# Row statistics in two GpSimd instructions an iteration, and six tiles of rows normalised on ScalarE

## What is computed

```python
x = x + xattn(layernorm(x), ctx)          # 16 heads, 8-bit q, k, v and probabilities
x = x + ffn(layernorm(x))                 # router on the normalised rows, 8 experts

def layernorm(x, eps=1e-05):
    m = mean(x, axis=-1); v = var(x, axis=-1)
    return (x - m) / sqrt(v + eps)
```

## Time and profile before

| | us |
|---|---|
| median of 3 runs (766.38 to 767.51) | 767.23 |
| the profiled execution | 768.47 |
| its span, first to last instruction | 766.6 |
| TensorE busy | 634.3 (83%) |
| VectorE busy | 580.2 (76%) |
| ScalarE busy | 448.7 (59%) |
| GpSimd busy | 379.6 (50%) |
| granted TensorE clock, mean | 0.967 |

### The profile page before, as it was taken

How to read it: one execution, slowest core, us unless ns; L and a number is a source line. 1 busy time by engine, 2 the same in 40 slices (tenths; PEclk the granted TensorE clock), 3 DMA queues, 4 the chain that set the end, 5 groups by cost and what they waited for, 6 DMA issues and landing times.

```text
span 766.6 us, 16055 instructions
## 1 busy us (share of the span) xinstructions
PE 634.3 (83%) x5281; PEld 328.8 (43%) x5281; DVE 580.2 (76%) x999; ACT 448.7 (59%) x532; POOL 379.6 (50%) x409
## 2 busy tenths in 40 slices
PE   5999899666776767676777678789999999999993
PEld 1434343233433434243434346355555555555551
DVE  4877698999998999989999999867447356465430
ACT  5243237588898888878887987415434344344321
POOL 4255344645557575766666764023453354344403
PEclk8999999999999999999999999799999999999997
DMA  8868767799998979899998988438787967977804
GB/s 229 227 135 192 155 146 116 146 170 181 162 182 158 216 152 215 164 212 176 184 184 176 194 178 154 107 100 231 219 220 185 240 156 199 231 179 222 141 13 54
DMA packets 330657, 132.28 MB, mean 173 GB/s; under 512 B 305140, under 2 KB 305140, under 8 KB 330616
## 3 DMA queue, kind: packets, MB, share of 16 engines
q1 hardware_dynamic: 323440, 115.53, 70.3%
q0 software_dynamic: 7168, 16.26, 10.2%
q10 hardware_dynamic: 8, 0.01, 0.0%
HBM read 44.33 MB, written 12.06 MB: 74 GB/s over the span
## 4 chain that ended last, share of the span: by engine, by line
PE 37%; issue 20%; DVE 16%; DMA 9%; POOL 6%; SPq 4%; ACT 3%; DVEq 1%; POOLq 1%; another core or an unknown queue 1%; ACTq 0%
PE psum L1435 31%; DMA work<-work 5%; DVE spare L1178 4%; PE psum L1551 3%; DMA keys_region<-values_region 2%; SPq L332 2%; DVE spare L1169 2%; ACT work L879 1%; POOL work L630 1%; SPq L436 1%; PE psum L1608 1%; PE psum L1513 1%; DMA work<-in_ctx_dram 1%; DVE values_region L1029 1%; POOL work L607 1%
## 5 line engine op out<-in xcount | busy, mean ns | idle before, releaser
L879 ACT ACTIVATE work<-spare,exp_bias 128x2048 int16<-128x2048 f32 (+1 forms) x128 | 255.7, 1998 | 51.8 <-DVE exp_bias L1187 46.3
L1178 DVE TENSOR_SCALAR_CACHE_REDUCE spare<-psum,q_step_now 128x1024 f32<-128x1024 f32 x128 | 162.9, 1281 | 10.6 <-PE psum L1551 10.4
L607 POOL CAST work<-work 128x2048 int16<-128x2048 uint8 x63 | 118.9, 1893 | 84.5 <-DMA work<-work 71.2
L1169 DVE TENSOR_SCALAR_CACHE_REDUCE spare<-psum,q_step_now 128x2048 f32<-128x2048 f32 x64 | 150.8, 2356 | 1.0 <-PE psum L1551 0.9
L1551 PE MATMUL psum<-keys_region,work 128*128 128x512 f16 x256 | 74.8, 394 | 46.8 <-DVE spare L1178 27.2
L708 POOL DMA_INDIRECT work<-x_rows,slot_tok x32 | 50.2, 1569 | 108.1 <-DVE slot_w L1367 75.1
L1551 PE MATMUL psum<-keys_region,bias_hl 128*128 128x512 f16 x256 | 73.1, 394 | 28.5 <-DVE spare L1178 24.0
L1513 PE MATMUL psum<-values_region,work 128*128 128x32 f16 x2048 | 71.0, 177 | 21.1 <-POOL work L607 12.9
L720 POOL DMA_INDIRECT out_dram<-keys_region,slot_tok x32 | 51.7, 1616 | 73.7 <-ACT keys_region L953 66.7
L1513 PEld LDWEIGHTS psum<-values_region,work 128*128 128x128 f16 x2048 | 67.1, 96 | 45.1 <-DMA work<-work 17.6
L1435 PE MATMUL psum<-work,spare 128*128 128x480 f16 (+1 forms) x396 | 79.2, 360 | 2.7 <-DVE work L1344 2.7
(11 more groups left out here) (217 smaller groups left out, 994.5 us busy)
## 6 DMA issues: line engine op xcount, KB each, us to landing
spare<-in_L_ffn_Wd_dram SPq DMA_DIRECT2D x8, 1024.0 KB
spare<-in_L_ffn_Wg_dram SPq DMA_DIRECT2D x7, 1024.0 KB
spare<-in_L_ffn_Wu_dram SPq DMA_DIRECT2D x7, 1024.0 KB, 11.5
work<-in_ctx_dram SPq DMA_DIRECT2D x3, 1024.0 KB, 6.5
work<-work SPq DMA_TRANSPOSE x185, 3.8
resid<-in_x_dram SPq DMA_DIRECT2D x2, 1024.0 KB, 8.9
x_rows<-work SPq DMA_DIRECT2D x8, 256.0 KB, 2.3
out_dram<-work SPq DMA_DIRECT2D x8, 256.0 KB, 2.5
```

Source lines behind the costliest of these rows:

```text
L607: nc.gpsimd.tensor_copy(p_T_int[h % 4 // 2], pair_bytes[h % 4 // 2]).then_inc(unpacked, 1)
L879: nc.scalar.activation(last_int[h % 2] if words and h >= H - 2 else p_int[h % 4], scores, ACT.Exp, bias=exp_bias[:, h % 4:h % 4 + 1], scal ...
L1169: nc.vector.tensor_scalar(staged[h % 4], psum[:, at:at + 4, :].rearrange("p b k -> p (b k)"), q_step_now[:, h:h + 1], None, ALU.mult, ALU.min,
L1178: nc.vector.tensor_scalar(staged[h % 4][:, 1024 * c:1024 * c + 1024], psum[:, at:at + 2, :].rearrange("p b k -> p (b k)"), q_step_now[:, h ...
```

## The change

`deviation` no longer calls `rsqrt_steps`. A Newton step is two instructions: t = y y v, then y = (t - 3 s^2) y, where s is a number known when the program is built that carries the factor left out; s changes in each step, and the last two instructions divide by it. `tensor_scalar` takes y or v from memory as its scalar operand. After the three steps GpSimd writes, without a wait between, `x1_scale` = y/s and `x1_mean` = -mean y/s. The function `normalise` on GpSimd is gone. `normalise_rows` on ScalarE, behind head 4's exponential, waits for both and computes scale x + bias over 128 x 512 with `ACT.Identity`. The step count per tile is 9 instead of 14 and now includes the sum of the row sums in `add_rows`, whose own semaphore is replaced by the step semaphore.

```diff
-            norm_steps = 14
+            norm_steps = 9
...
-                nc.gpsimd.tensor_tensor(x1_mean[:, :], proj_sum[:, :], row_sum[:, bass.ds(j, 1)], ALU.add).then_inc(rows_summed, 1)
+                own = Steps(pool, pool_step, norm_base + norm_steps * j, passed)
+                own.mark(nc.gpsimd.tensor_tensor(x1_mean[:, :], proj_sum[:, :], row_sum[:, bass.ds(j, 1)], ALU.add))
                 nc.gpsimd.tensor_tensor(x1, x1, row(j), ALU.add).then_inc(x1_added, 1)
-                pool.wait_ge(rows_summed, j + 1)
+                own.after(own.n)
...
-                own = Steps(pool, pool_step, norm_base + norm_steps * j, passed)
-                own.link(nc.gpsimd.tensor_scalar(ln1_var[:, :], x1_square[:, :], 1.0 / D, LN_EPS, ALU.mult, ALU.add))
-                rsqrt_steps(own, ln1_var[:, :], ln1_y[:, :], ln1_t[:, :])
-                assert own.n == norm_steps
-
-            def normalise(j):
-                pool.wait_ge(mean_ready, j + 1)
-                passed()
-                nc.gpsimd.tensor_scalar(x1_norm, x1, x1_mean[:, :], ln1_y[:, :], ALU.subtract, ALU.mult).then_inc(x1_normed, 1)
+                own = Steps(pool, pool_step, norm_base + norm_steps * j + 1, passed)
+                var, y, t = ln1_var[:, :], ln1_y[:, :], ln1_t[:, :]
+                own.link(nc.gpsimd.tensor_scalar(var, x1_square[:, :], 1.0 / D, LN_EPS, ALU.mult, ALU.add))
+                own.link(nc.gpsimd.tensor_scalar(y.bitcast(I32), var.bitcast(I32), -0.5, float(RSQRT_GUESS), ALU.mult, ALU.add))
+                scale = 1.0
+                for _ in range(3):
+                    own.link(nc.gpsimd.tensor_scalar(t, y, y, var, ALU.mult, ALU.mult))
+                    own.link(nc.gpsimd.tensor_scalar(y, t, 3.0 * scale ** 2, y, ALU.subtract, ALU.mult))
+                    scale = -2.0 * scale ** 3
+                assert own.n == norm_steps - 1
+                nc.gpsimd.tensor_scalar(x1_scale[:, :], y, 1.0 / scale, None, ALU.mult).then_inc(norm_ready, 1)
+                nc.gpsimd.tensor_scalar(x1_mean[:, :], x1_mean[:, :], y, -1.0 / scale, ALU.mult, ALU.mult).then_inc(norm_ready, 1)
...
-                if after_rows:
-                    normalise(i - 2)
...
+            def normalise_rows(j):
+                act.wait_ge(norm_ready, 2 * j + 2)
+                nc.scalar.activation(x1_norm, x1, ACT.Identity, bias=x1_mean[:, 0:1], scale=x1_scale[:, 0:1]).then_inc(x1_normed, 1)
+
...
+                    if h == 4 and after_rows:
+                        normalise_rows(i - 2)
```

More of the change, by code:

```diff
@@ L216, in xattn_moe @@
         ln1_mv = sb("ln1_mv", [P, 2])
-        ln1_var, ln1_y, ln1_t = (sb(n, [P, 1]) for n in ("ln1_var", "ln1_y", "ln1_t"))
+        ln1_var, ln1_y, ln1_t, x1_scale = (sb(n, [P, 1]) for n in ("ln1_var", "ln1_y", "ln1_t", "x1_scale"))
         g_inh, g_dist, g_w, g_zone, g_fb, g_tmp, g_rank, g_best = (
@@ L269, in xattn_moe @@
         att_taken, att_ready, att_cut, attT_in = (sem(n) for n in ("att_taken", "att_ready", "att_cut", "attT_in"))
-        sums_inverted, steps_ready, rows_summed, mean_ready, x1_squared, bias_summed = (sem(n) for n in ("sums_inverted", "steps_ready", "rows_summed", "mean_ready", "x1_squared", "bias_summed"))
+        sums_inverted, steps_ready, norm_ready, mean_ready, x1_squared, bias_summed = (sem(n) for n in ("sums_inverted", "steps_ready", "norm_ready", "mean_ready", "x1_squared", "bias_summed"))
         proj_full, proj_out, x1_added, x1T_in = (sem(n) for n in ("proj_full", "proj_out", "x1_added", "x1T_in"))
```

## The result

| | before | after |
|---|---|---|
| median, us | 766.81 (4 runs, 765.09 to 767.51) | 754.76 (4 runs, 753.72 to 755.51) |
| ratio | | 0.9845, 95% interval 0.9822 to 0.9868 |
| profiled execution, us | 768.47 | 755.5 |
| its span, us | 766.6 | 753.7 |
| mean granted TensorE clock | 0.967 | 0.976 |

12.05 us faster, where 8.6 were forecast.

A forecast was written before the change was run, and what follows sets the result against it. VectorE was taken to bound the attention tiles, with 10.7 us of idle time to win in tiles 2 to 7. Less 2.1 us that stays, the gain is 8.6: 759.9 from the profiled 768.47, 758.6 against the median; range 755.4 to 763.5.

The forecast's parts named there:

- The bound: Attention tiles 2 to 7: VectorE sets the pace, and only its idle time, 10.7 us, can be won.
- the chain behind the stall: Before head 9's second half: VectorE waits for TensorE, that for SyncE's transposed attention half, that for late GpSimd; six stalls, 9.36 us.
- The statistics: GpSimd's row statistics: 14 chained steps become 8 plus two unchained, a gain of 1.6 us a tile.
- the dear bound: GpSimd statistics: steps with operands from memory cost 0.08 us more than 0.38, leaving a gain of 1.2 us.
- SyncE next: After GpSimd, SyncE is late next: tile 4's attention half issues behind head 4's transpose, 2.7 us earlier, not 3.7.
- ScalarE: Moved normalise between exponentials of heads 4 and 5: 0.7 us, bounds 0.6 to 0.8, covered by 0.58 idle; path cost 0.
- What stays: VectorE idle time left in tiles 2 to 7: 0.5 us in three tiles plus 0.6 at tile 6's start, 2.1 us.
- Rival (a): SyncE becomes the pace in the six tiles: only 4 to 6 us gained, about 762 us; chance 0.22.
- (b): GpSimd's chain not really shorter, or another release right behind: gain 0 to 1.4, 766.5 us; chance 0.09 shared with (d).
- (d): ScalarE table loads at exp/identity switches, two of 1.28 us a tile: gain about 0.2 a tile, 766; chance 0.09 shared with (b).
- (c): ScalarE's new in-order wait for a late scale bites beyond about 3 us of lateness; 14 us slower, 781 us; chance 0.07.
- The rule against the change: Skill page: add and multiply belong on VectorE, not ScalarE; the prediction set it aside because VectorE has no idle time here.

The follow-up runs named there:

- fill: Kernel before the change, with 14 throwaway matmuls of 256 columns in TensorE's pause before the values of head 2, tiles 1 to 7: 767.22 us, ratio 1.0017.
- move_only: Kernel before, with only the normalise moved to ScalarE; Newton steps keep four instructions, and two more write scale and bias: 756.11 us, ratio 0.9873.
- delay4: Changed kernel with four linked 128 x 128 copies on GpSimd behind the scale and bias, in front of head 0's unpacking: 763.77 us, ratio to before 0.9957.
- early_slot: Changed kernel with the normalise on ScalarE behind head 2's exponential instead of head 4's: 764.60 us, ratio to before 0.9984.
- slack2: Changed kernel with two linked 128 x 128 copies on GpSimd between head 0's unpacking and the attention half: 755.38 us, ratio to before 0.9882.
- slack4: Changed kernel with four linked 128 x 128 copies on GpSimd between head 0's unpacking and the attention half: 758.37 us, ratio to before 0.9926.
- dve_norm: Changed kernel with the normalise on VectorE, behind head 5's second half, instead of on ScalarE: 764.30 us, ratio to before 0.9972.

## Why the prediction was right or wrong

**The bound, and the chain behind the stall: right.** VectorE's idle time was what could be won, and it was won. GpSimd's lateness made the stall: each part that makes it earlier shrinks it, 0.9 us more on it is free, and 1.85 us more brings a stall back in five of six tiles.

**The statistics: sign right, size off.** 1.6 us forecast, 1.0 measured. A step with operands from memory costs 0.50 to 0.55 us (0.29 to 0.34 and 0.21 between), not the 0.46 of the dear bound. It cost nothing: SyncE, not GpSimd, came last, as said.

**SyncE next: right.** Issue at 318.39, directly behind head 4's transpose; the move of the lead is 2.7 us, as worked out.

**ScalarE: right.** 0.80 us, the upper bound and not the 0.7 I took, in the 0.58 us of cover and the overlap; no wait. The price worked out from the Trainium skill ("ScalarE: Activation LUTs", "What ACT_TABLE_LOAD costs"), an estimate of 0.80, was the better one, and the trace agrees with it: 0.80.

**What stays: the step that failed.** I kept 2.1 of 10.7 us: 0.5 in each of three tiles for a half-clock stretch, and 0.6 at the start of tile 6. The number of stretches was wrong, not their price.

- I took the stretches as given and carried their rate over to the changed kernel. Most of them go with TensorE's pauses, which the change takes away. With the pause filled the profile has none while the stall is there (fill); with the pause gone there are none in move_only and one and two in the changed kernel, against five and six in the kernel before; with a pause elsewhere they appear there (delay4, six of six tiles). It is a tendency and not a rule: of the six pauses of 1.3 to 2.1 us in the kernel before only two had a stretch behind them, one of 1.9 had none, and early_slot has five stretches behind pauses of 0.8 to 1.1. What decides in a single tile is open.
- The price was about right. Where a stretch came in the changed kernel, it left 0.32 to 0.45 us of idle time, for the 0.5 I took. But in tiles 2 to 7 there was one, and what is left there in all is 0.41 us, and 0.32 in the second profile.
- I put the start of the projection at 325.2 on the old time scale; it came 2.05 us before need, at 324.9. At half clock that makes a stall of 0.3 where I had 0.6, a small error to the same side.

With 0.4 instead of 2.1 the sum had been 756.9. The other 2 us lie outside it. In tiles 2 to 7 the time fell by 11.65 us, 1.3 more than 10.7 less 0.4. Of that 0.3 is idle time in the last part that the sum had not listed; VectorE is also busy 0.8 us less in the five tiles (196.13 to 195.31) and 0.25 less in the last part. Most of this belongs to the stalls. Two instructions of VectorE that follow without a stall overlap by 0.09 us (323.14 + 0.15 against 323.20), and at each of the eight stalls of the five tiles this was lost; in numbers, from the reciprocal to the need at head 9 it is 11.16 us in tile 4 before and 11.06 after. So a stall cost 0.1 us more than its idle time. The rest, tile 1's 0.6 and the experts' 1.0, is not explained by the change. Tile 1 is chance, as its second profiles show. The experts, from the last reciprocal on, took 289.1 us in both profiles of the kernel before and also in move_only, and 288.2 and 288.5 in the two of the changed kernel; over all twelve profiles it is 288.2 to 290.0 (slack2 288.3, slack4 290.0, which differ by two small copies a tile). A difference of 1 us there can be the spread of the executions.

**The range.** Its low end was said to be the whole idle time and half a microsecond more. From 767.23 that is 756.0; the 755.4 that I wrote stands 11.8 below it. What the range lacked is the 0.1 us a stall, which the rows could have given, and a share for the spread of the parts that the change doesn't touch, such as the 1 us of the experts.

**Rival (a), SyncE as the pace: wrong.** Its arithmetic of waits held, its premise did not. Its last step was also miscounted: 39.5 and 40.1 us a tile are 9.6 and 6 us gained in six tiles, not 4 to 6. SyncE waits 12.1 us in six tiles for 22.0 before, 2.0 a tile where 1.9 was forecast; but the transposes did not get dearer, a median of 1.77 us in tile 4 against 1.74. Tile 1's 1.87 was no price of speed. The waits for exponentials became more frequent, 21 for 15, so SyncE is caught up with ScalarE more often than before.

```profile
SPq L308 <- ACT work L885: 11.6, 21, 0.9
SPq L308 <- POOL work L599: 0.5, 1, 0.5
```

**(b) and (d): wrong.** Ten instructions at up to 0.55 us are far from 0.72 each; there is still one table load. **(c): didn't happen**, but early_slot shows that its threshold was too generous. I gave ScalarE's lateness 3 us before it costs more than the old stall; 2.3 us in front of head 3 cost nearly all of it.

**The rule against the change** (the Trainium skill, "ScalarE: Activation LUTs", "Rules for kernel authors": use VectorE, not ScalarE) would have lost 9 to 10 us here (dve_norm). I had priced VectorE's form at 0.54 and it was 1.23.

## What to carry to other kernels

When one late hand-over stalls the pacing engine once a round, measure the lead that it needs, here 3.8 us from issue to use, and compare the change with that: what brings the lead over the edge takes the whole stall, and what comes after it is free and brings nothing. A slow stretch of the clock behind a pause that the change removes may go with the pause: put the sum with it and without it into the range. Single stalls of a loop differed from one profile of the same kernel to the next (0.20 to 2.72 us here) while their sum stayed within 0.2 us: predict from the sum over the rounds, and take a second profile before a single tile's number carries an argument.

## What the runs showed of the hardware

- GpSimd, one column: an instruction with immediates or two tensors lasts 0.19 to 0.24 us; a `tensor_scalar` with two operands from memory beside its input 0.34, with one 0.26 to 0.31. Fewer instructions, each dearer by more than half: six of them for twelve save 1.0 us net of the two that are added, not half of the time.

```profile
L629 POOL TENSOR_SCALAR ln_t<-ln_y,ln_var 128x1 f32<-128x1 f32 x18 | 6.1, 341 | 3.8 <-POOL ln_y L630 2.5 <-POOL ln_y L626 1.3
L630 POOL TENSOR_SCALAR ln_y<-ln_t,ln_y 128x1 f32<-128x1 f32 x18 | 5.3, 295 | 3.8 <-POOL ln_t L629 3.8
```

- An fp32 `tensor_scalar` of 128 x 512 from SBUF to SBUF on VectorE that began during GpSimd's cast ended 0.28 to 0.29 us after it, in six of six tiles, and took 1.23 us on average for 0.54. The Trainium skill, "SBUF — State Buffer", "SBUF: two separate sides", says that the pair of ports that the two engines share is an exclusive lock, held for the whole instruction by whichever starts first, where VectorE's instruction is in a mode with two ports. The trace agrees with a lock; no run shows the mode. VectorE's scores, which come from PSUM, took 2.34 us each there and 2.36 in the kernel before.
- TensorE's granted clock fell to 0.50, which is 1.2 GHz, behind many of its pauses of 1.3 to 2.1 us in the attention (two of six in one profile of the kernel before, six of six in delay4), behind some of 0.8 to 1.1 us (five tiles of early_slot), and stayed at 1.00 in tiles 1 to 7 when throwaway matmuls filled the pause. At 0.50 the way from SyncE's issue to VectorE took 4.80 us for 3.77.
- Successive VectorE instructions overlapped by 0.09 us; a stall cost that in addition to its idle time.
